# Smaller strips of the systolic array for three small products of a fused graph-attention, linear-attention and mixture-of-experts kernel, and a new order of its steps

## What is computed

```python
x = x + conv(groupnorm(x))          # layer 0, per image
t = tokens(x)                       # layer 1, 256 tokens of 256 channels per image
t = t + linear_attention(layernorm(t))
t = t + moe(layernorm(t))           # 16 experts, 4 chosen, and a shared expert

# in conv, temporal attention
E = softmax(V_e @ sigmoid(lhs @ rhs + b_e), axis=1)        # 16 x 16 per image
x_tat = einsum('bnfj,bjt->bnft', x, E)
# spatial attention: a product of two narrow factors, 256 x 16 and 16 x 256
lhs2 = einsum('bnft,t->bnf', x_tat, W1) @ W2
rhs2 = einsum('f,bnft->btn', W3, x_tat)
S = softmax(V_s @ sigmoid(lhs2 @ rhs2 + b_s), axis=1)      # 256 x 256 per image
out = sum_k einsum(cheb[k] * S, x) @ Theta[k]

# in the attention, causal over the 256 tokens, 16 heads of 16 channels
S = S + pk_t[..., :, None] * v_t[..., None, :]; z = z + pk_t
out_t = (pq_t @ S) / (pq_t . z + eps)
```

## Time and profile before

| what | value |
|---|---|
| three runs: median, lowest, highest | 931.17, 930.77, 931.88 us |
| the profiled execution's own time | 933.24 us |
| its span | 931.3 us |
| mean granted clock of TensorE | 0.989 |
| busy: TensorE, VectorE, ScalarE, GpSimd | 892.2, 623.1, 445.6, 228.6 us |
| matmul records | 7824 |
| share of the chain that ended last: TensorE | 83% |

### The profile page before, as it was taken

The page is one execution under the profiler, slowest core; times in us unless marked ns, Lnnn a source line. Parts: engine busy times, 40 slices in busy tenths (PEclk is TensorE's granted clock), DMA queues, the critical chain, the costliest instruction groups (busy, mean ns, idle before and its releaser), DMA issues.

```text
span 931.3 us, 19454 instructions
## 1 busy us (share of the span) xinstructions
PE 892.2 (96%) x7824; PEld 787.5 (85%) x7824; DVE 623.1 (67%) x1637; ACT 445.6 (48%) x845; POOL 228.6 (25%) x198
## 2 busy tenths in 40 slices
PE   5998788999999999999999999999999999999997
PEld 3676666998988989889898989888898898998997
DVE  6456876887697468864797467963788547864522
ACT  3443444552574436743565526744466424732432
POOL 2013200123311224112421234112241134122232
PEclk9998899999999999999999999999999999999999
DMA  7000230030002010111002010010102100120121
GB/s 234 1 2 1 65 131 1 1 103 28 23 19 79 25 46 13 40 58 34 25 12 73 25 45 24 25 61 23 46 13 59 39 13 24 37 72 26 37 67 34
DMA packets 37961, 39.21 MB, mean 42 GB/s; under 512 B 5232, under 2 KB 34416, under 8 KB 37872
## 3 DMA queue, kind: packets, MB, share of 16 engines
q1 hardware_dynamic: 37872, 37.96, 13.0%
HBM read 32.97 MB, written 4.98 MB: 41 GB/s over the span
## 4 chain that ended last, share of the span: by engine, by line
PE 83%; DVE 8%; ACT 4%; issue 2%; DMA 1%; POOL 0%; SPq 0%; POOLq 0%; DVEq 0%; ACTq 0%
PE ring L1365 9%; PE d_ps L521 5%; PE g_ps L521 4%; PE d_ps L523 4%; PE d_ps L522 4%; PE g_ps L523 4%; PE u_ps L523 4%; PE g_ps L522 4%; PE u_ps L522 4%; PE u_ps L521 4%; PE ring L1233 4%; PE num L1262 3%; PE ring L521 3%; PE ring L1348 3%; PE ring L523 3%; PE ring L522 3%
## 5 line engine op out<-in xcount | busy, mean ns | idle before, releaser
L707 POOL TENSOR_TENSOR hl<-hb,hh 128x512 fp32r<-128x512 f32 x96 | 126.0, 1313 | 424.4 <-ACT hh L838 424.4
L838 ACT ACTIVATE hh<-hb 128x512 fp32r<-128x512 f32 x96 | 60.7, 632 | 143.5 <-DVE hb L1205 119.0
L1200 DVE TENSOR_TENSOR hb<-sl,u_ps 128x512 f32<-128x512 f32 x88 | 60.3, 685 | 93.3 <-issue 37.6
L521 PE MATMUL d_ps<-hh,down_h 128*128 128x256 f32 x384 | 116.6, 304 | 2.7 <-POOL hl L707 2.7
L522 PE MATMUL d_ps<-hl,down_h 128*128 128x256 f32 x384 | 107.8, 281 | 0.0
L523 PE MATMUL d_ps<-hh,down_l 128*128 128x256 f32 x384 | 107.6, 280 | 0.0
L521 PE MATMUL g_ps<-normed_h,gate_h 128*128 128x256 f32 x352 | 105.7, 300 | 1.1 <-DVE hb L1200 0.8
L1087 DVE TENSOR_TENSOR shared<-ring,constants 128x512 f32<-128x512 f32 x128 | 79.4, 683 | 34.1 <-PE ring L1233 34.1
L523 PE MATMUL g_ps<-normed_h,gate_l 128*128 128x256 f32 x352 | 99.2, 282 | 0.0
L523 PE MATMUL u_ps<-normed_h,up_l 128*128 128x256 f32 x352 | 99.0, 281 | 0.0
L522 PE MATMUL u_ps<-normed_l,up_h 128*128 128x256 f32 x352 | 98.8, 281 | 0.0
(11 more groups left out here) (401 smaller groups left out, 2134.7 us busy)
## 6 DMA issues: line engine op xcount, KB each, us to landing
weights_over_hidden<-weights_by_expert SPq DMA_DIRECT2D x128, 128.0 KB, 3.0
shared<-denominators_by_head SPq DMA_DIRECT2D x16, 256.0 KB
out_x<-kept SPq DMA_DIRECT2D x16, 256.0 KB, 2.2
x_s<-in_x SPq DMA_DIRECT2D x12, 256.0 KB, 3.1
raw_weights<-in_gateT SPq DMA_DIRECT2D x4, 384.0 KB, 7.1
raw_weights<-in_upT SPq DMA_DIRECT2D x4, 384.0 KB, 6.2
raw_weights<-in_down SPq DMA_DIRECT2D x4, 384.0 KB, 9.1
cheb_s<-in_cheb SPq DMA_DIRECT2D x3, 256.0 KB, 5.6
```

Of the source, the lines that this page charges most:

```text
L521: eng.matmul(ps, wh, xh, start=start, stop=False, **how)
L707: pool.tensor_tensor(hl[:, j % 2, :], hb, hh[:, j % 2, :].bitcast(F32), ALU.subtract).then_inc(*ffn_pool.mark(p, f"lo{j}"))
L838: act.activation(hh[:, j % 2, :], hb, ACT.Copy).then_inc(*ffn_act.mark(p, f"hi{j}"))
L1200: dve.tensor_tensor(hb, sl, gate_up(p, j)[1][:, :], ALU.mult).then_inc(*ffn_dve.mark(p, f"h{j}"))
```

## The change

Erep's two images go to the row strips at partitions 0 and 64 and to a bank each. W1 and the identity come from memory at both places instead of being put together by VectorE. VectorE writes eTx in two instructions and reads Erep in four. For p2, ScalarE also copies the right factor's rows to the left's place and the other way round (`l3`), so that four matmuls sit in four row strips and four banks; VectorE adds b_s in four instructions of 128 x 256. kv becomes 16 matmuls of 32-column weights by 32 moving columns in four column strips, of one quarter of the former output; the mask's instruction reads it by broadcast. All three strings of the list of steps are written anew.

```diff
-    +1 tok0 tok1 lg +1 gn +1 nrm +3 xg +1 r1 xl0 xl1 xT0 +1 r2 M +2 k0 xT1 k1 r3 +2 Y0 +1 prod v1 silu r4
+    +1 tok0 tok1 lg +1 gn +1 nrm +4 xg r1 xT0 xl0 +1 xl1 r2 M xT1 +2 k0 k1 +1 r3 +1 silu Y0 +1 prod v1 r4 cb
...
-    return [f"{name}_{j}" for j in range({"S": 4, "Y": 4, "p2": 2}.get(name if name == "p2" else "" if name == "rd" else name[0], 0))] or [name]
+    return [f"{name}_{j}" for j in range({"S": 4, "Y": 4, "p2": 4, "Erep": 2}.get(name if name in ("p2", "Erep") else "" if name == "rd" else name[0], 0))] or [name]
...
-                    "Epre": [(conv_dve, "esub")], "Erep": [(conv_dve, "WE")], "lr": [(conv_act, "r21")],
+                    "Epre": [(conv_dve, "esub")], "lr": [(conv_act, "l31")],
...
+            READ_OUT["Erep_" + b] = [(conv_dve, "WE" + b)]
+            for m in BI:
+                READ_OUT[f"p2_{2 * int(b) + int(m)}"] = [(conv_dve, f"pb{b}{m}")]
...
                     for b in range(2):
-                        act.activation(g.r2[64 * b:64 * b + T, :], t[64 * b + 32:64 * b + 32 + T, 0:N], ACT.Copy).then_inc(*conv_act.mark(p, f"r2{b}"))
+                        low, high = slice(64 * b, 64 * b + T), slice(64 * b + 32, 64 * b + 32 + T)
+                        act.activation(g.r2[low, 0:P], t[high, 0:P], ACT.Copy).then_inc(*conv_act.mark(p, f"r2{b}"))
+                        act.activation(g.r2[high, :], t[low, 0:N], ACT.Copy).then_inc(*conv_act.mark(p, f"l3{b}"))
...
-                    dve.tensor_tensor(g.eTx, g.eT[:, :, :].unsqueeze(3).to_broadcast([T, 2, T, T]),
-                                      g.emax[:, :].unsqueeze(2).to_broadcast([T, 2, T]).unsqueeze(3).to_broadcast([T, 2, T, T]), ALU.mult).then_inc(*cv.mark(p, "ET"))
+                    for b in range(2):
+                        dve.tensor_tensor(g.eTx[64 * b:64 * b + T], g.eT[:, b, :].unsqueeze(2).to_broadcast([T, T, T]),
+                                          g.emax[:, b:b + 1].unsqueeze(2).to_broadcast([T, T, T]), ALU.mult).then_inc(*cv.mark(p, f"ET{b}"))
...
+                        for m in range(2):
+                            dve.tensor_tensor(g.th[:, b, m], tile(p, f"p2_{2 * b + m}")[:, 0:N], bs_s[:, m], ALU.add).then_inc(*cv.mark(p, f"pb{b}{m}"))
...
+                    for c in range(2):
+                        for b in range(2):
+                            rows = slice(64 * b, 64 * b + T)
+                            last = pe.matmul(tile(p, f"Erep_{b}")[:, 32 * c:32 * c + 17], g.eTx[rows, 8 * c:8 * c + 8].rearrange("p j f -> p (j f)"), small_at("iw1")[rows, 0:17],
+                                             start=True, stop=True, tile_position=(64 * b, 0))
...
+                    for b in range(2):
+                        for m in range(2):
+                            rows = slice(64 * b + 32 * m, 64 * b + 32 * m + T)
+                            right, left = (g.l2[rows, P:N], g.r2[rows, :]) if m else (g.r2[rows, 0:P], g.l2[rows, :])
+                            last = pe.matmul(tile(p, f"p2_{2 * b + m}")[:, 0:N], right, left, start=True, stop=True, tile_position=(64 * b + 32 * m, 0))
...
+                            for j in range(4):
+                                heads_of = v_s[:, b, 0, 4 * c + j, :].rearrange("p (s e) -> p s e", e=16)[:, 0:3:2, :]
+                                last = pe.matmul(t[32 * j:32 * j + 32, 32 * q:32 * q + 32].rearrange("p (s e) -> p s e", s=2), ktok[:, q * P + 32 * j:q * P + 32 * j + 32], heads_of,
+                                                 start=True, stop=True, tile_position=(0, 32 * j))
```

More of the change, by code:

```diff
@@ L125 @@
[L125 to L133, removed]
+    0:gn 0:high0 0:xg 0:hot0 0:xT0 1:gn 0:M 0:xT1 0:hot1 0:hot2 1:xg 0:high1 0:hot3 0:Y0 0:hot4 1:xT0 0:hot5
+    2:gn 0:prod 1:M 0:hot6 1:xT1 0:Epre 0:Eexp 1:Y0 0:Erep 1:prod 0:lr 0:low0 1:Epre 2:xg 0:p2 2:xT0 1:Eexp
@@ new lines @@
+    0:sp0 0:rv0 1:Erep 0:hot7 0:sp1 0:st0 1:lr 0:hot8 0:rv1 2:M 0:Y1 0:st1 0:o0 0:o1 1:p2 0:tc0 0:high2 1:sp0
+    1:rv0 0:tc1 1:sp1 1:st0 0:hot9 2:xT1 0:xb 0:hot10 2:Y0 0:z1 0:hot11 0:hot12 2:prod 1:rv1 1:Y1 0:low1 0:z2
+    0:z3 1:st1 1:o0 0:tok0 2:Epre 0:tok1 0:nrm 2:Eexp 1:o1 0:xl0 0:xl1 1:tc0 1:xb 1:tc1 2:Erep 1:z1 0:k0 0:k1
+    0:v1 0:q0 0:v0 0:kt 2:lr 1:z2 0:high3 0:q1 2:p2 0:dent 0:kv 0:hot13 0:hot14 0:rd 0:hot15 1:z3 0:low2
+    0:S00 2:sp0 0:hot16 0:V00 2:rv0 0:S01 2:sp1 0:high4 2:st0 0:at0 0:V01 0:high5 2:rv1 0:hot17 0:high6 0:S10
@@ new lines @@
+    0:V10 0:low3 0:low4 0:S11 0:hot18 0:low5 0:hot19 0:high7 0:high8 0:hot20 0:V11 2:Y1 0:at1 0:low6 0:wo0
+    0:wo1 0:tk0 0:hot21 0:tk1 0:high9 0:high10 0:nrm2 2:st1 2:o0 0:hot22 0:xn0 0:xn1 0:low7 0:high11 0:low8
+    1:tok0 1:tok1 0:lg 0:low9 0:hot23 +2 1:nrm 0:r1 2:o1 0:low10 0:r2 +1 2:tc0 0:r3 1:xl0 0:silu 1:xl1
+    0:low11 +1 0:r4 0:cb +1 1:k0 1:k1 +1 1:v1 1:q0 +1 1:v0 0:high12 1:kt 1:q1 0:low12 +1 1:dent 1:kv +2 1:rd
+    0:high13 +1 0:low13 1:S00 +2 0:exp +2 1:V00 +2 1:S01 +2 2:tc1 +2 1:at0 2:xb 1:V01 1:S10 +2 2:z1 +2 1:V10
@@ L134 @@
+    1:S11 +2 +2 1:V11 +1 1:at1 2:z2 +1 1:wo0 +3 1:wo1 +2 1:tk0 1:exp +4 1:tk1 +2 1:nrm2 +2 2:z3 +2 1:xn0
+    1:xn1 +1
 """
 BODY = """
-    +1 tok0 tok1 lg +1 gn +1 nrm +3 xg +1 r1 xl0 xl1 xT0 +1 r2 M +2 k0 xT1 k1 r3 +2 Y0 +1 prod v1 silu r4
-    Epre cb Eexp q0 v0 kt q1 +2 Erep dent +1 kv lr rd +2 S00 +2 V00 S01 +1 p2 at0 +1 V01 S10 +2 sp0 +1 rv0 +1
-    sp1 st0 +1 rv1 Y1 +2 st1 +1 o0 +2 V10 +1 S11 +2 o1 tc0 tc1 xb +1 z1 +1 V11 +2 at1 z2 +2 wo0 wo1 +2 tk0
-    exp tk1 +5 nrm2 z3 +1 xn0 xn1 +1
+    +1 tok0 tok1 lg +1 gn +1 nrm +4 xg r1 xT0 xl0 +1 xl1 r2 M xT1 +2 k0 k1 +1 r3 +1 silu Y0 +1 prod v1 r4 cb
@@ L141 @@
+    Epre Eexp q0 v0 kt q1 +1 Erep +1 dent kv rd +1 lr +2 S00 +2 p2 +2 V00 S01 +1 sp0 rv0 at0 V01 S10 +2 sp1
+    +1 st0 +1 rv1 V10 Y1 +3 st1 xb o0 o1 +1 tc0 tc1 +2 z1 +1 S11 +3 V11 +2 at1 z2 +2 wo0 wo1 exp +2 tk0 tk1
+    +2 nrm2 +3 z3 +1 xn0 xn1 +1
 """
 CLOSING = """
-    +1 7:tok0 7:tok1 +2 7:nrm +1 6:lg +1 7:xl0 7:xl1 6:r1 6:r2 +2 7:k0 +1 6:r3 6:silu +1 6:r4 6:cb 7:k1 7:v1
-    7:q0 +1 7:v0 +2 7:kt 7:q1 +3 7:dent 7:kv 7:rd +3 7:S00 +3 7:V00 +1 7:S01 +2 7:at0 +2 7:V01 7:S10 +4 7:V10
-    7:S11 +2 7:V11 +2 7:at1 7:wo0 +3 7:wo1 +2 7:tk0 7:tk1 +5 7:nrm2 7:xn0 7:xn1 +3 7:lg +1 7:r1 +3 7:r2 +3
@@ L147 @@
-    7:r3 +1 7:silu 7:r4 +1 7:cb +30 7:exp +17
+    +1 7:tok0 7:tok1 +1 7:nrm +2 6:lg +2 6:r1 7:xl0 7:xl1 6:r2 +3 7:k0 6:r3 6:silu 6:r4 6:cb 7:k1 7:v1 +3
+    7:q0 7:v0 7:kt 7:q1 +3 7:dent 7:kv +2 7:rd +1 7:S00 +2 7:V00 7:S01 +2 7:at0 +2 7:V01 7:S10 +3 7:V10 7:S11
+    +3 7:V11 +1 7:at1 +1 7:wo0 7:wo1 +2 7:tk0 +1 7:tk1 +3 7:nrm2 +3 7:xn0 7:xn1 +2 7:lg +1 7:r1 +4 7:r2 +4
+    7:r3 +1 7:silu 7:r4 7:cb +21 7:exp +29
 """
```

69 lines of the change are left out of this document (28 added, 41 removed).

## The result

| kernel | median, lowest, highest | ratio to before, 95% interval |
|---|---|---|
| before | 930.97, 927.44, 931.88 us (4 runs) | |
| changed | 941.2, 937.66, 943.84 us (4 runs) | 1.0115, 1.007 to 1.0159 |

A forecast was written before the change was run, and what follows sets the result against it. TensorE's own time and its waits were taken as the bound. Turns -6, opening -8 and closing -2.2 sum to -16.2 us: 917.0 on the profiled execution, 915 us as median; range 905 to 927, forecast's own 907 to 921.

The forecast's parts named there:

- The opening: Opening: shorter small steps and matmuls covering VectorE's normalization chains, less a later Y0, give -8 us (-15 to +2).
- Work: ... Sum -4.7: Opening: TensorE's work shrinks by 2.2 us for Erep, 2.1 for p2 and 0.4 for kv.
- The 1.9 us that were to come back: Opening: pair 1's second filter product, 7.11 us, would run at full clock in 5.2; part of a gain counted half.
- Rival (1): Opening: its two gaps are replaced by as long ones, since VectorE's chain sets the pace; 922 us, chance 0.15.
- Rival (2): Turns: p2 needs all four banks of S00 back and delays eat the gain; 0.4 us to spare, 921 us, chance 0.08.
- The turn: One turn of BODY: shorter small steps and changed waits give -1.2 us, five turns -6 (-2 to -11).
- the 0.1 of borders: Turn: one excursion out of the ffn's matmuls fewer, so two borders saved, 0.1 us less (0 to 0.2).
- The waits: Turn: new waits at S00 and S10 cost 0.3 us each; the wait at xn goes, 0.5 less.
- The closing: Closing: cb three ffn steps earlier removes most of TensorE's wait for GpSimd's low part; -2.2 us with kv (-3 to 0).
- Rival (3): Opening: more hot steps before Y0 raise TensorE's clock early, 6 us less, 909 us; chance 0.10.
- Rival (4): Opening: late Y0 and pauses keep pair 0's filter products at the low clock, 20.7 us more, 936 us; chance 0.08.
- Both signs named for being wrong: Turns staying above 107 us, or the clock row having more than two slices at 8, would show the forecast wrong.

The follow-up runs named there:

- e3: The changed kernel with SyncE sending and fetching back pair 0's denominators before the ten late weight loads; 932.73 us, ratio 1.0031 to before.
- f2: The kernel before with only p2's edit (four row strips, four banks, more copies and sums), old lists; 942.57 us, ratio 1.0133.
- f4: The kernel before with its old Erep, p2 and kv, in the three new lists of steps; 942.52 us, ratio 1.0124.
- g4: The changed kernel with kv's matmuls ordered strip by strip, four in a row in one strip; 951.01 us in one run.
- f1: The kernel before with only kv's edit (16 matmuls in four column strips), old lists; 930.92 us, ratio 0.9998.

## Why the prediction was wrong

- **The opening is where it failed**, at two steps. "The new list puts pair 1's filter product between tok1 and xl0 ..., so that 5.2 and some 7 us of matmuls cover these chains": the waits of 2.25 and 4.08 left these two places, and the bracketed waits up to pair 2's attention (without the first, for the input) still grew from 22.9 to 40.0 us. The largest new one, 9.79, comes from a step that I followed on VectorE and not on SyncE: z3 of pair 1, moved behind rd of pair 0, frees ten loads that SyncE issues ahead of rd's transfers. e3 showed it, 8.5 us. And "Work: ... Sum -4.7" (its 2.2 for Erep adds up to 2.3) took every microsecond of TensorE in the opening as one of the path, where f2 shows that p2's edit alone brings 5.5 us of waits there. The 1.9 us that were to come back because 86.69 would run at full clock did not: pair 1's two products of that kind took 6.70 and 6.66 us, for 5.45 and 7.11.
- **Rival (1), gaps replaced by as long ones**, was given 0.15 and came in part: in place of the 4.08 before lr of pair 2 stand 4.43 before p2, for the same kind of small instructions on VectorE. The new list brings them without any edit, in f4 at dent:

```profile
114.66 1.08 PE L1436 MATMUL ring<-shared,constants 128*32 128x128 f32 x16 [4.10 <-DVE shared L1066]
```

- **Rival (2), the ring of four banks**, had the right mechanism and was given 0.08, but was thought through for the turns alone. Its margin of 0.4 us was worked out for the new list with S00's banks, and there it holds (no wait before p2 at 406.45). Behind S01 in the old list the wait is 1.09 us, and in the opening of f2 up to 2.02. What it cites on reading out stands in that page of the Trainium skill (TensorEngine Tiling (Array Packing)) under PSUM Bottleneck; here the price was the wait before the product.
- **The turn** was to be 1.2 us shorter and is 0.21. The work was undersized: Erep 0.44 for 0.49, p2 0.42 for 0.52, kv 0.68 for 0.19, dent 0.12 for the 0.1 of borders, 1.66 in all for 1.3. With 1.23 us more of waits 0.43 were left, and 0.21 arrived. kv was priced by small matmuls that had stood in one strip: g4 gives 0.025 there, as the 0.028 taken. The estimate from the Trainium skill (TensorEngine Tiling (Array Packing), Instruction Overhead), 0.80 us, is met by g4 and missed by half when the strips take turns.
- The waits: S00 0.35 for 0.3 and S10 0.47 for 0.3 as foretold, xn gone as foretold. Not foretold: Erep ahead of gu3, 0.54; tok1 and a dn step for GpSimd, 0.15 and 0.21. The step that failed is "So in the turns only TensorE's own time and what it waits for count": a TensorE that waits 0.42 us in a turn can still be one that arrives just in time at its next steps. f1 shows it, with 0.80 us saved and 0.73 us more of waits.
- **Y0** of pair 0 starts at 18.81 us, 1.4 later, for the forecast 1.3.
- **The closing** gained 0.6 for 2.2. I took the wait of 2.2 us for that of the low part at 886.75; the timeline has it at 926.17, in the last dn step, where GpSimd's last low part has nothing to hide behind. No list moves it: 2.16 in both kernels.
- **Rival (3), the early rise of the clock**, came and hid part of the loss: Y0 of pair 1 takes 1.17 us, at full level, where it took 2.09 before (both rows below). Up to kv of pair 2 TensorE's time outside its waits fell from 253.4 to 244.3 us. Three pairs at 1.66 us make 5.0 of these 9.1; the rest I put down to the clock, an estimate.
- **Rival (4), the low level through pair 0's filter products**, was not it: they ran at full level, both in 10.63 us from 49.81 on, as before in 5.34 each. But the kernel is slower, for which the forecast had 0.08.
- Both signs named for being wrong came: a turn above 107, and more than two slices at 8.

```profile
25.85 2.09 PE L1247 MATMUL ring<-theta_s,raw_weights 32*128 32x128 f32 x32 [0.59 <-DVE shared L939]
```

```profile
25.79 1.17 PE L1252 MATMUL ring<-theta_s,raw_weights 32*128 32x128 f32 x32 [0.69 <-DVE shared L939]
```

The waits of the closing, before and with the change:

```profile
926.17 0.39 PE L521 MATMUL d_ps<-hh,down_h 128*128 128x256 f32 x1 [2.16 <-POOL hl L707]
```

```profile
933.01 0.39 PE L522 MATMUL d_ps<-hh,down_h 128*128 128x256 f32 x1 [2.16 <-POOL hl L708]
```

## What to carry to other kernels

Where one list orders all engines and was laid by hand until TensorE hardly waits, a shorter matmul step can be worth nothing until the chains that end at the next steps are shorter too: subtract the saving, then ask of each step behind it what it waits for and since when that has been running. How much arrives depends on the list: of kv's saving nothing in the old BODY (f1), 0.37 of 0.40 us in the new (g4). A split over row strips is paid in banks, and most of the price stands before the split step itself, which now waits for the tiles just ahead of it in the ring. When a step is moved, follow what it frees on the DMA issuing queue, and what small transfer stands behind that.
